# Scale steps of the second norm moved from GpSimd to VectorE, weight products joined, in a Mamba-like block with an int8 product

## What is computed

```python
def _s6(x, A_log, D, x_proj_w, dt_proj_w, dt_proj_b):
    A = -jnp.exp(A_log)
    xp = jnp.einsum('bld,ed->ble', x, x_proj_w)
    ...
    delta = jax.nn.softplus(jnp.einsum('blr,dr->bld', d_rank, dt_proj_w) + dt_proj_b)
    deltaA = jnp.exp(jnp.einsum('bld,dn->bldn', delta, A))
    deltaB_u = jnp.einsum('bld,bln,bld->bldn', delta, Bm, x)
    def step(h, inp):
        dA_t, dBu_t, C_t = inp
        h = dA_t * h + dBu_t
        y = jnp.einsum('bdn,bn->bd', h, C_t)
        return (h, y)
...
def _xla_quantized_matmul(x2d, weight_q, weight_scale):
    amax = jnp.max(jnp.abs(x2d), axis=-1, keepdims=True)
    x_scale = jnp.maximum(amax, EPS) / 127.0
    x_q = jnp.clip(jnp.round(x2d / x_scale), -128, 127).astype(jnp.int8)
    acc = jax.lax.dot_general(x_q, weight_q, (((1,), (1,)), ((), ())), preferred_element_type=jnp.int32)
    return acc.astype(jnp.float32) * x_scale * weight_scale[None, :]
...
x = x + _L0_attn_ref(_layernorm(x, axis=-1), ...)
x = x + _L0_ffn_ref(_layernorm(x, axis=-1), ...)
```

## Time and profile before

| what | value |
|---|---|
| median of 3 runs | 2826.95 us (2826.89 to 2827.49) |
| span of the profiled execution, first to last instruction | 2824.8 us |
| granted TensorE clock, mean | 0.998 of full speed |
| busy: PE, DVE, ACT, POOL | 2778.3 (98%), 2721.6 (96%), 2729.4 (97%), 2762.4 us (98%) |
| share of the chain that ended last: POOL, issue, PE | 61%, 32%, 4% |
| length of one chunk in the middle of the run | 86.5 us |
| instructions | 59754 |

### The profile page before, as it was taken

How to read it: one execution, slowest core, us unless ns; L and a number is a source line. 1 busy time by engine, 2 the same in 40 slices (tenths; PEclk the granted TensorE clock), 3 DMA queues, 4 the chain that set the end, 5 groups by cost and what they waited for, 6 DMA issues and landing times.

```text
span 2824.8 us, 59754 instructions
## 1 busy us (share of the span) xinstructions
PE 2778.3 (98%) x22624; PEld 2515.1 (89%) x22624; DVE 2721.6 (96%) x2801; ACT 2729.4 (97%) x5084; POOL 2762.4 (98%) x1137
## 2 busy tenths in 40 slices
PE   7999999999999999999999999999999999999998
PEld 6899899898998898998989989989989899899897
DVE  6999999999999999999999999999999999999997
ACT  7999999999999999999999999999999999999995
POOL 4999999999999999999999999999999999999998
PEclk9999999999999999999999999999999999999999
DMA  5334544444444345444444444453544544445432
GB/s 189 91 98 95 136 114 116 124 102 107 118 123 115 100 102 132 112 121 121 94 118 116 125 112 104 102 132 110 123 113 93 128 116 118 116 106 119 100 95 63
DMA packets 197312, 319.11 MB, mean 113 GB/s; under 512 B 93025, under 2 KB 93025, under 8 KB 180642
## 3 DMA queue, kind: packets, MB, share of 16 engines
q1 hardware_dynamic: 164290, 250.29, 29.1%
q0 software_dynamic: 32736, 65.02, 15.1%
HBM read 212.70 MB, written 102.56 MB: 112 GB/s over the span
## 4 chain that ended last, share of the span: by engine, by line
POOL 61%; issue 32%; PE 4%; DMA 1%; DVE 0%; ACT 0%; SPq 0%; POOLq 0%; DVEq 0%
POOL A L532 47%; POOL C L549 5%; POOL C L541 3%; POOL XN L484 2%; POOL out L556 1%; POOL out L564 1%; PE Y L777 1%; POOL PW L501 1%; PE PB L755 1%; PE PB L752 1%; PE Y L773 0%; SPq L402 0%; DVE A L913 0%; PE PM L817 0%; POOL RO L503 0%
## 5 line engine op out<-in xcount | busy, mean ns | idle before, releaser
L532 POOL TENSOR_TENSOR A<-A,CB 128x2048 f32<-128x2048 f32 x511 | 2348.9, 4721 | 40.1 <-DMA CB<-c_rows 27.5
L913 DVE TENSOR_TENSOR_SCAN A<-A,CAR,PB 128x512 f32<-128x512 f32 x1536 | 1844.7, 1259 | 23.6 <-PE PB L752 13.1
L595 ACT ACTIVATE A<-DEL,an 128x512 f32<-128x512 f32 x2048 | 1376.3, 719 | 0.4
L777 PE MATMUL Y<-idf,A 128*128 128x128 f32 x8192 | 1125.8, 273 | 2.2 <-POOL A L532 1.8
L777 PEld LDWEIGHTS Y<-idf,A 128*128 128x128 f32 x8192 | 945.7, 141 | 83.1 <-issue 67.2
L616 ACT ACTIVATE DB<-XN,BC 128x512 f32<-128x512 f32 x1472 | 1003.1, 719 | 1.1 <-PE PB L755 1.1
L755 PE MATMUL PB<-idf,DB 128*128 128x128 f32 x5888 | 857.9, 274 | 24.3 <-DVE A L913 18.6
L755 PEld LDWEIGHTS PB<-idf,DB 128*128 128x128 f32 x5888 | 683.7, 142 | 55.1 <-DVE A L913 37.2
L913 DVE TENSOR_TENSOR_SCAN A<-A,PB 128x512 f32<-128x512 f32 x512 | 591.1, 1203 | 28.0 <-PE PB L752 13.4
L752 PEld LDWEIGHTS PB<-DG,XN 128*128 128x128 f32 x4608 | 565.6, 192 | 42.4 <-issue 32.4
L752 PE MATMUL PB<-DG,XN 128*128 128x128 f32 x4608 | 600.0, 275 | 2.4 <-DVE A L913 2.4
(11 more groups left out here) (96 smaller groups left out, 1652.2 us busy)
## 6 DMA issues: line engine op xcount, KB each, us to landing
CB<-c_rows SPq DMA_DIRECT2D x128, 1024.0 KB, 5.9
DG<-b_diag SPq DMA_DIRECT2D x160, 256.0 KB, 5.8
X<-in_x SPq DMA_DIRECT2D x31, 1024.0 KB, 5.7
out<-bib SPq DMA_DIRECT2D x31, 1024.0 KB, 8.6
out<-X POOLq DMA_DIRECT2D x31, 1024.0 KB, 9.4
out<-C POOLq DMA_DIRECT2D x31, 1024.0 KB, 9.0
b_diag<-DG SPq DMA_DIRECT2D x2, 1280.0 KB, 11.0
b_diag<-BC SPq DMA_DIRECT2D x160, 2.0 KB, 5.7
```

The lines of the kernel that those rows point to most:

```text
L532: gp.tensor_tensor(A[s % NA][:, :, :], A[s % NA][:, :, :], CB[:, s % (4 * NG), :].unsqueeze(1).broadcast_to([128, KB, L]), ALU.mult).then_ ...
L595: act.activation(A[s % NA][:, g, :], DEL[k % 2][:, g, :], ACT.Exp, scale=an[:, g, n:n + 1])\
L777: i = pe.matmul(Y[j][:, g * 128:(g + 1) * 128], A[s % NA][:, g, j * 128:(j + 1) * 128], idf[:, :], is_transpose=True, start=False, stop=(n ...
L913: dve.tensor_tensor_scan(A[s % NA][:, g, :], A[s % NA][:, g, :], PB[(4 * s + g) % NPB][:, :], init, ALU.mult, ALU.add).then_inc(s_scan, 1)
```

## The change

Four things are changed.

1. The four instructions of ascale and the step move from POOL to DVE, as five tasks: quot (PW3 = PW1 * UNIT^2 * RO3), heron (RO1 = PW3 + RO2), step, unit (AM0 = RO0 * RO1) and floor (AM1 = max(AM0, TINY)). The factor UNIT = 1/(254*D) is drawn into root (as UNIT^2 under the logarithm) and quot, so RO1 is in units of the output scale. scales is now the reciprocal of RO1, and step is AM3 = min(RO0/TINY, AM2). So step no longer depends on unit and floor, which feed scale_a alone.
2. scale_p is one instruction of 128x2048, with the weight scale read again for each tile. It waits for all four scale_a.
3. The rounding constant is laid down by a product of 128 rows, ones times 12582912/128, instead of one row. The two tiles have 128 partitions.
4. PLACES is new for nearly all tasks; FIRST stays, LAST gets entries for the new tasks.

```diff
@@ PLACES (one row of many)
-        "du": (-340, -199, -168, -148),
+        "du": (-73, -69, -66, -62),
...
+    UNIT = 1.0 / (254.0 * D)
+    TINY = 1e-6 / 127.0
...
-        one = sb("one", [1, 128], bf16)
-        big = sb("big", [1, D], bf16)
+        one = sb("one", [128, 128], bf16)
+        big = sb("big", [128, D], bf16)
...
-            gp.memset(big[:, :], MAGIC).then_inc(s_big, 1)
+            gp.memset(big[:, :], MAGIC / 128.0).then_inc(s_big, 1)
...
-            def ascale(p):
...
-                gp.tensor_tensor(PW[:, 3, :], PW[:, 1, :], RO[:, 3, :], ALU.mult).then_inc(s_qu, 1)
...
-                gp.tensor_tensor(RO[:, 1, :], PW[:, 3, :], RO[:, 2, :], ALU.add).then_inc(s_as, 1)
...
-                gp.tensor_tensor(AM[:, 0, :], RO[:, 0, :], RO[:, 1, :], ALU.mult).then_inc(s_z, 1)
...
-                gp.tensor_scalar(AM[:, 1, :], AM[:, 0, :], 2e-6 * D, 1.0 / (254.0 * D), ALU.max, ALU.mult).then_inc(s_zm, 1)
-
-            def step(p):
...
-                gp.tensor_tensor(AM[:, 3, :], AM[:, 2, :], RO[:, 0, :], ALU.mult).then_inc(s_st, 1)
...
-                gp.wait_ge(s_oa, T * p + j + 1)
+                gp.wait_ge(s_oa, T * (p + 1))
                 gp.wait_ge(s_w2, 64)
-                gp.tensor_tensor(C[:, j, :], C[:, j, :], wsb[:, :], ALU.mult).then_inc(s_op, 1)
+                gp.tensor_tensor(C[:, :, :], C[:, :, :], wsb[:, :].unsqueeze(1).broadcast_to([128, T, D]), ALU.mult)\
+                  .then_inc(s_op, 1)
...
-                act.activation(PW[:, 2, :], PW[:, 1, :], ACT.Ln, bias=eps[:, 1:2]).then_inc(s_la, 1)
+                act.activation(PW[:, 2, :], PW[:, 1, :], ACT.Ln, bias=eps[:, 1:2], scale=UNIT * UNIT).then_inc(s_la, 1)
...
+            def quot(p):
+                dve.wait_ge(s_ir, p + 1)
+                dve.scalar_tensor_tensor(PW[:, 3, :], PW[:, 1, :], UNIT * UNIT, RO[:, 3, :], ALU.mult, ALU.mult)\
+                   .then_inc(s_qu, 1)
+
+            def heron(p):
+                dve.wait_ge(s_qu, p + 1)
+                dve.tensor_tensor(RO[:, 1, :], PW[:, 3, :], RO[:, 2, :], ALU.add).then_inc(s_as, 1)
+
+            def scales(p):
+                dve.wait_ge(s_as, p + 1)
+                dve.reciprocal(AM[:, 2, :], RO[:, 1, :]).then_inc(s_k, 1)
+
+            def step(p):
+                dve.wait_ge(s_k, p + 1)
+                dve.wait_ge(s_pv, p + 1)
...
+                dve.scalar_tensor_tensor(AM[:, 3, :], RO[:, 0, :], 1.0 / TINY, AM[:, 2, :], ALU.mult, ALU.min)\
+                   .then_inc(s_st, 1)
+
+            def unit(p):
...
+                dve.tensor_tensor(AM[:, 0, :], RO[:, 0, :], RO[:, 1, :], ALU.mult).then_inc(s_z, 1)
+
+            def floor(p):
...
+                dve.tensor_scalar(AM[:, 1, :], AM[:, 0, :], TINY, 1.0, ALU.max, ALU.mult).then_inc(s_zm, 1)
```

More of the change, by code:

```diff
@@ L30 @@
+        442, 497, 519, 568, 568, 568, 588, 588, 593, 691, 691, 720, 720, 720, 720, 720, 726, 726, 726, 784,
+        784, 803, 835, 841, 843),
+        "delta": (-401, -380, -331, -312),
+        "dl_t": (-320, -206, -163, -143),
+        "du": (-73, -69, -66, -62),
+        "floor": (1782,),
+        "gather": (1145, 1222, 1222, 1222),
+        "heron": (1333,),
         "idle": (2244, 2663, 2696, 3192),
-        "inv": (1473,),
+        "inv": (1332,),
         "last_p": (25000, 25001),
@@ L74 @@
-        "xn_p": (-818, -794, -779),
-        "xp_out": (-475,),
+        "q_mm": (2047, 2062, 2120, 2122),
+        "q_t": (1884, 1981, 1992, 2033),
+        "qt_out": (2006, 2007, 2017, 2032),
+        "quot": (1332,),
+        "root": (1350,),
+        "rstd0": (-982,),
+        "scale_a": (2046, 2090, 2098, 2104),
+        "scale_out": (20000, 20001, 20002, 20003),
+        "scale_p": (2129,),
+        "scales": (1336,),
+        "scan": (26, 28, 28, 28, 30, 54, 71, 124, 139, 157, 205, 205, 205, 316, 316, 316, 327, 327, 327, 327,
@@ new lines @@
+        327, 327, 327, 327, 327, 330, 330, 331, 332, 334, 334, 336, 338, 338, 338, 338, 342, 402, 504, 639,
+        639, 693, 807, 807, 807, 807, 807, 809, 809, 809, 816, 884, 909, 909, 909, 927, 931, 936, 945, 953,
+        953, 954, 975, 976),
+        "shift0": (-1074,),
+        "square": (1302, 1305, 1305, 1305),
+        "stats0": (-2026, -2026, -1939, -1396),
+        "step": (1337,),
+        "store_c": (-241,),
+        "store_g": (-377,),
[8 rows of a table added]
+        "times_c": (-67, 264, 359, 441, 460, 500, 500, 566, 910, 910, 910, 910, 915, 915, 915, 927),
@@ L76 @@
+        "unit": (1635,),
+        "var1": (1338,),
+        "weights": (-475,),
+        "x_p": (-516, -515, -504, -502),
+        "x_t": (-576, -568, -541, -532),
+        "xn": (-901,),
+        "xn_p": (-1047, -938, -897),
+        "xp_out": (-603,),
         "xt_d": (-1484, -1483),
-        "xt_out": (-705, -658, -626, -603),
+        "xt_out": (-760, -702, -668, -664),
 }
@@ L124 @@
         819, 821, 825, 826, 872),
+        "floor": (5450,),
         "gather": (2316, 2748, 3224, 3261),
+        "heron": (5410,),
         "idle": (6076, 6407, 6408, 7994),
@@ L142 @@
         "square": (1919, 2064, 2284, 2328),
-        "step": (7913,),
+        "step": (5430,),
         "tb": (-14, 1, 12, 35, 49, 60, 107, 111, 120, 125, 153, 163, 166, 174, 206, 230, 244, 252, 266, 271,
@@ L152 @@
         "times_c": (119, 281, 385, 428, 452, 471, 502, 525, 538, 581, 692, 723, 880, 891, 893, 1055),
+        "unit": (5440,),
         "var1": (3546,),
@@ L990, in _ @@
             run(last_v=last_v, xt_d=xt_d, stats0=stats, aggr0=lambda p, i: aggr(p), gather=gather, du=du, amax=lambda p, i: amax(p),
-                scale_out=scale_out, inv=lambda p, i: inv(p), scales=lambda p, i: scales(p),
+                scale_out=scale_out, inv=lambda p, i: inv(p), quot=lambda p, i: quot(p), heron=lambda p, i: heron(p), scales=lambda p, i: scales(p),
+                step=lambda p, i: step(p), unit=lambda p, i: unit(p), floor=lambda p, i: floor(p),
                 weights=lambda p, i: weights(p), last_q=last_q, scan=scan)
```

105 lines of the change are left out of this document (33 added, 72 removed), and 16 rows, old and new, of the table PLACES.

## The result

The changed kernel takes 3183.25 us (3182.16 to 3183.42, 4 runs) beside 2827.22 us (2826.89 to 2828.58) for the kernel before on the same chip: ratio 1.126, 95% interval 1.124 to 1.127. The forecast was 3045 with a range to 3160. The direction and the kind of cause were right; the size was too small by more than a third (218 us expected, 356 found), and the time lies 23 us outside the range.

A forecast was written before the change was run, and what follows sets the result against it. GpSimd was taken to bound at 86.5 us a chunk. VectorE would need 84.57 + 0.7 + 8.0 + 0.3 = 93.6, so 31 x 7.1 = 220 more, edges -1, giving 3045 us; range 2890 to 3160.

The forecast's parts named there:

- What binds, and that time on VectorE counts at once: Whole chunk: GpSimd binds at 86.5 us; added VectorE time counts at once beyond about 1.3 us in chunks with carries.
- Two SBUF tensors are held by a GpSimd product: Quotient, sum, step and unit on VectorE, 4 columns: each waits out GpSimd's product under way, 0 to 4.52 us.
- the floor: VectorE's one-tensor scale floor: nothing in the sum for a hold, possible range 0 to 2.3 us a chunk.
- the term "held": Waits of quotient, sum, step and unit on VectorE for GpSimd's products: 8.0 us a chunk, taken as the mean.
- the waits: VectorE's remaining waits in each chunk: 0.3 us.
- The argument from the tail: Tail centring, one tensor, 541 ns against 677 for a two-tensor sum: like operations may read both ports and be held.
- the walk: One pass through the new order, chunk with carries: quotient held 2.9, sum 3.1, step free, unit 3.1; sum 9.1.
- rival (3): A held VectorE operation loses GpSimd's next turn as well: 12 a chunk, period 97.6, time 3170; chance 0.07.
- a period above 96 would speak for lost turns: Sign in the profile of after: a chunk period above 96 us would mean held VectorE operations lose GpSimd's next turn.
- TensorE -1.0 a chunk: Rounding constant's product over 128 rows instead of one: four save 1.0 us a chunk, TensorE about 85.1.
- GpSimd -2.3 a chunk: Scale chain 1.65 and step 0.2 off GpSimd, joined weight product 4.5 instead of 5.0: its work falls to 84.2.
- The no-hold cases at 2814 or 2824: No VectorE operation held: 2814, 86.1 a chunk, chance 0.11; or 2824, 86.4 a chunk without TensorE's gain, chance 0.05.

The follow-up runs named there:

- m2_transfers: Separate small program: one VectorE 4-column sum among GpSimd products of 4x512 tiles, some behind GpSimd transfers; behind a transfer 16.96 and 27.19 us, to the last product's end.
- e5_floor_column: Changed kernel with only the floor written as four one-column operations: 3148.20 us.
- e2_on_gpsimd: Changed kernel with quotient, sum, unit, floor, step and second reciprocal back on GpSimd in the old forms, rest of the change kept: 2839.99 us, ratio 1.005.
- e3_one_input: Changed kernel with each of the five VectorE steps as four one-column operations, any second tensor as per-partition scalar: 2843.53 us, ratio 1.006.
- m1_hold: Separate small program: GpSimd multiplies 128x2048 tiles, VectorE issues one small operation into the first; sum of two 4-column SBUF tensors 3.72 us, alone 0.16.

## Why the prediction was right, and where it was wrong

- **What binds, and that time on VectorE counts at once:** right. VectorE is busy in 98.17 of 98.20 us.
- **Two SBUF tensors are held by a GpSimd product, at four columns as at 512:** right, and shown alone (3.72 against 0.16) and in place (3183 against 2844 with the same numbers in a form that isn't held). The Trainium skill ("SBUF — State Buffer", "Who interferes with whom") has the second of the two wait until the first is finished. That agrees with the products' ends while they stand clear of each other; behind a transfer the hold ran over six products in m2_transfers (27.19 us), and there the measurement decides.
- **What failed is the size of two terms of the sum, 93.6 where 98.1 was measured.** Of the 4.5 us a chunk the floor has 2.3, the term "held" 1.8 and the waits 0.4 (0.7 for 0.3). Times 31 that is 139 us, and 3045 + 139 = 3184 is the result. The mechanism was right, these sizes were not.
- **The floor was put at nothing, and that is the larger part.** It measured 2.42, its upper bound of 2.3 above its own work; the range had it only as a bound. The argument from the tail (a tensor_scalar at 541 ns beside a sum at 677) compared lengths without GpSimd and said nothing about a hold. The Trainium skill ("VectorE: DVE Perf Modes", "Mode 2×_2P — use both read ports for one tensor") had it the other way, and the runs agree with it: four columns 3.65, one column 0.15. In e5_floor_column, where the floor is not held, 35 of these 71 us came out of the time: what an operation stands is not what its removal gives back.
- **"Held" was put at 8.0.** The four operations it counts measured 4.80 + 2.49 + 2.95 + 0.13 = 10.4, which is 9.8 above their own work of 0.6. 1.1 of the 1.8 missing were in the forecast's own hand: the walk gave 9.1, and the mean of 8.0 was taken because it "needs no exact phase". But the phase repeats from chunk to chunk. The sum and the unit (walked 3.1 each) were near, the step (0) was right, and the quotient (walked 2.9) was not: in an ordinary chunk it stood 4.1, since it came 0.9 us into a product that was recorded 4.9 long, and not 1.6 into one of 4.5.
- **The lost turn of rival (3)**, to which I gave 0.07, is real, but only in every fourth chunk, and there the rows show no extra price. The quotient has 8.4 us in these chunks instead of 4.1. The sum then goes free (0.13 instead of 3.4) and the unit stands 1.7 instead of 3.5, so the five together have 12.8 us against 13.7 in the others. The forecast's sign "a period above 96 would speak for lost turns" misled: the period is above 96 by the floor and the phase.
- **TensorE -1.0 a chunk:** right in size (0.65 for 0.90), worth nothing, as the forecast had it in principle.
- **GpSimd -2.3 a chunk:** half of it. Its busy time fell by 1.1 (86.25 to 85.13), not to 84.2, among other things because its products with C are recorded 16 us longer in all (2348.9 to 2364.9). The joined product saves 0.45, of which its transfer's wait takes back 0.35, and a piece that waits for several tiles can lose 1.9.
- **The no-hold cases at 2814 or 2824** were not tested. e2_on_gpsimd (2840) has the steps on GpSimd, and e3_one_input (2844) pays 2.5 us a chunk on the engine that binds for what would be 0.7. What both show is that the last interval is some 7 us longer in the new order (87.2 and 87.9 us; before 80.3), with GpSimd waiting for VectorE's scans; the forecast had -1 for the edges.
- **Range:** short by 23 us. Above 3045 it had room for the floor's 71 us and 44 more; the term "held" took 56 and the waits 12.

## What to carry to other kernels

Before a small step moves from GpSimd to VectorE, count its SBUF tensors and its columns: with two tensors, or four fp32 columns in a tensor_scalar, it costs what is left of GpSimd's product (2.4 to 4.8 us here), and behind a GpSimd transfer it can cost everything GpSimd has ready (17 us and more in m2_transfers). Where such an operation falls repeats from chunk to chunk, so walk it through the order and take what the walk gives, not a mean. If it must run there, write it one column at a time with the second tensor as per-partition scalar (0.2 us each), or put one side in PSUM (0.16 us in m1_hold, not tried in the kernel), and look in the trace for short operations whose ends coincide with another engine's.
An engine that is not the bound may be worth slowing: one wait of GpSimd for itself gave 85 us back, most of it by the place at which the quotient then came to lie. And joining pieces on the engine that binds saves 0.1 us a piece but waits for the last of them.
